# A recommendation tower: gathers released by step counts, 32x128 unit matmuls, and an opening whose ids are spread by matmuls

## What is computed

```python
e = jnp.stack([tbl_0[ids[:, 0]], ..., tbl_39[ids[:, 39]]], axis=1)
xi = inputs[:, iidx, :]
xj = inputs[:, jidx, :]
out = jnp.einsum('bpd,pde,bpe->bp', xi, bilinear_matrices, xj)
...
h = jnp.concatenate([z, dense_ctx], axis=1)
h = jnp.maximum(h @ W_top1 + b_top1, 0.0)
h = jnp.maximum(h @ W_top2 + b_top2, 0.0)
y = h @ W_top3
```

## Time and profile before

| | us |
|---|---|
| median of 3 runs | 1214.42 |
| span of the profiled execution | 1229.4 |
| PE busy | 958.3 (78%) |
| DVE busy | 556.3 (45%) |
| POOL busy | 470.2 (38%) |
| ACT busy | 175.3 (14%) |
| chain that ended last: PE | 73% |
| the same: "issue" | 16% |
| the same: another core or an unknown queue | 7% |

### The profile page before, as it was taken

The page is one execution under the profiler, slowest core; times in us unless marked ns, Lnnn a source line. Parts: engine busy times, 40 slices in busy tenths (PEclk is TensorE's granted clock), DMA queues, the critical chain, the costliest instruction groups (busy, mean ns, idle before and its releaser), DMA issues.

```text
span 1229.4 us, 30049 instructions
## 1 busy us (share of the span) xinstructions
PE 958.3 (78%) x13844; PEld 463.2 (38%) x13844; DVE 556.3 (45%) x652; ACT 175.3 (14%) x432; POOL 470.2 (38%) x502
## 2 busy tenths in 40 slices
PE   5136768878968778777788877888788877887998
PEld 4012334423435334433244323443234422344556
DVE  5013336524736445543255433553345623445782
ACT  3100001111102111211001110012101121012211
POOL 7745342453142442335422454226532265222000
PEclk9556687888878899889787887888888888888999
DMA  5006000010000100001000100001000000000000
GB/s 132 14 18 214 8 10 6 8 37 8 5 9 6 36 10 6 8 12 33 9 7 6 36 10 10 6 7 37 10 9 6 6 13 10 8 6 6 3 3 1
DMA packets 28094, 24.32 MB, mean 20 GB/s; under 512 B 11525, under 2 KB 25793, under 8 KB 27841
## 3 DMA queue, kind: packets, MB, share of 16 engines
q0 software_dynamic: 15616, 8.03, 4.3%
q1 hardware_dynamic: 11738, 13.87, 3.5%
q10 hardware_dynamic: 616, 0.51, 0.1%
HBM read 22.31 MB, written 0.06 MB: 18 GB/s over the span
## 4 chain that ended last, share of the span: by engine, by line
PE 73%; issue 16%; another core or an unknown queue 7%; ACT 2%; DVE 1%; SPq 1%; ACTq 0%; DMA 0%
PE Y L634 25%; PE ZL L654 23%; PE ZL L680 14%; PE H L610 8%; PE H L589 2%; ACT xcols L763 1%; PE Y L689 1%; DVE one L863 0%; PE Y L698 0%; PE H L593 0%; SPq L489 0%; ACTq L472 0%; PE H L689 0%; DMA tab<-tbl 0%
## 5 line engine op out<-in xcount | busy, mean ns | idle before, releaser
L560 POOL DMA_INDIRECT rows<-tbl,idx x488 | 468.7, 961 | 645.9 <-PE H L589 447.3
L894 DVE TENSOR_TENSOR prod<-Y,xcols 128x1024 f32<-128x1024 f32 x336 | 400.2, 1221 | 518.6 <-remote 399.4
L634 PE MATMUL Y<-xcols,mats 32*64 32x256 f32 x6400 | 334.6, 429 | 72.3 <-issue 40.8
L654 PE MATMUL ZL<-prod,sel 128*32 128x256 f32 x3200 | 316.3, 421 | 65.3 <-issue 59.5
L634 PEld LDWEIGHTS Y<-xcols,mats 32*64 32x64 f32 x6400 | 171.2, 146 | 233.6 <-issue 204.5
L680 PE MATMUL ZL<-z,w_sb 128*32 128x256 f32 x1568 | 169.6, 421 | 33.8 <-issue 29.8
L654 PEld LDWEIGHTS ZL<-prod,sel 128*32 128x32 f32 x3200 | 114.6, 117 | 213.4 <-issue 175.0
L763 ACT ACTIVATE xcols<-H 32x256 f32<-32x256 f32 (+3 forms) x219 | 82.5, 377 | 523.9 <-PE H L589 264.5
L610 PE MATMUL H<-one,parts 125*32 125x256 bf16 x1668 | 99.4, 317 | 70.3 <-issue 69.1
L680 PEld LDWEIGHTS ZL<-z,w_sb 128*32 128x32 f32 x1568 | 63.1, 116 | 114.2 <-issue 89.2
L610 PEld LDWEIGHTS H<-one,parts 125*32 125x32 bf16 x1668 | 54.8, 105 | 116.6 <-issue 112.6
(11 more groups left out here) (48 smaller groups left out, 152.4 us busy)
## 6 DMA issues: line engine op xcount, KB each, us to landing
rows<-tbl,idx POOLq DMA_INDIRECT x488
idb<-ids_turned SPq DMA_DIRECT2D x7, 768.0 KB
w_sb<-w SPq DMA_DIRECT2D x1, 1792.0 KB
mats<-m_wide SPq DMA_DIRECT2D x22, 64.0 KB
mats<-m_wide SPq DMA_DIRECT2D x1, 1152.0 KB
mats<-m_wide SPq DMA_DIRECT2D x1, 960.0 KB
idb<-ids_turned SPq DMA_DIRECT2D x12, 64.0 KB
tab<-tbl SPq DMA_DIRECT2D x6, 112.0 KB
```

The lines of the kernel that those rows point to most:

```text
L560: pool.indirect_dma_start(out=rows[:, slot, t, D * q:D * (q + 1)], out_offset=None, in_=tables[f], in_offset=bass.IndirectOffsetOnAxis(ap= ...
L634: last = pe.matmul(Y[2 * D * c:2 * D * (c + 1), bank, cols], mats[D * r:D * (r + 1), u * P + 2 * D * c:u * P + 2 * D * (c + 1)], xcols[D * ...
L654: last = pe.matmul(Z[D * q:D * (q + 1), :], sel[:, GF * (SPAN - 1 - o):GF * (SPAN - 1 - o) + 32], prod[:, (2 * s + bank_of(k, q) // 2) % P ...
L894: dve.tensor_tensor(prod[:, half, :, :].rearrange("p b (u c) -> p b u c", c=BLK), Y[:, pair:pair + 2, :].rearrange("p b (u c) -> p b u c", ...
```

## The change

- **Gathers.** A table `gather_steps` gives each gather a step, and POOL waits for `s_y` to reach it before that one gather. From block 1 on the steps are 0.43 apart and not earlier than half a step after the slot's last turn. In block 0 the first 12 gathers are free, the next 6 wait for the first hot look-ups, and the others are spread between earlier turns. POOL still issues in the order of blocks and waves.
- **Unit matmuls.** In the 21 steps of a block that hold no diagonal slot, `multiply` uses 8 matmuls of 32 rows and 128 columns in place of 16 of 64. The 4 others stay as they were. Operands and results are the same.
- **The opening.** Block 0's ids are spread by matmuls: a column of ids, repeated 128 times, times an identity matrix in fp16 (`widen`), copied by ACT to `idb` (`spread`). DVE's order is new: first 10 one-hot slots, then table parts between the others. PE's first hot look-ups go part by part, and the other blocks' ids are turned in steps 1 and 2 as fills, copied by ACT and loaded behind step 3.
- **Loads.** `mats` comes in pieces of three units about five steps ahead, `w1` tile by tile in steps 10 to 22, `w2` and the rest in step 23, each behind a wait of SP for `s_y`; later blocks' ids come in three loads in place of one.

The core of the diff:

```diff
-LOADS = [(0, 3), (3, 5), (5, 10), (10, 16), (16, 22), (22, 40), (40, NU)]
-
-BY_UNIT = 5
+LOADS = [(0, 3), (3, 5)] + [(u, min(u + 3, NU)) for u in range(5, NU, 3)]
+
+BY_UNIT = 2
+
+AHEAD = 5
+SPREAD_AT = 3
+SPREAD_BY = SPREAD_AT + 3
+DENSE_AT, W1_AT, W2_AT = 8, range(10, 24, 2), 23
+W_DMAS = ZT + 4
+
+
+def load_step(k):
+
+    return max(min(SLOT_OF[u] for u in range(*LOADS[k])) // PAIR - AHEAD, 0)
...
+GATHER_EVERY, LANDS_IN = 0.43, 3.0
+FREE_WAVES = 3
+
+IDS_AT = [1, 1, 2, 2]
...
-FIRST_SLOTS = 23
+FIRST_SLOTS = HOT_RING
...
+def gather_steps():
+
+    waves = [(n, j) for n in range(NB) for j in range(len(cold(n)))]
+    turned = {("turn", n, j): 0.0 for n, j in waves}
+    turned.update({what: float(s) for s, step in enumerate(ITEMS) for what in step if what[0] == "turn"})
+    at, t = [], 0.0
+    for k, (n, j) in enumerate(waves):
+        if (n, j) == (1, 0):
+            t = 0.0
+        count = BT * len(cold(n)[j])
+        for i in range(count):
+            if n == 0 and j < FREE_WAVES:
+                t = -2.0
+            elif n == 0:
+                a, b = [turned["turn", 0, j - d] if j - d >= FREE_WAVES - 1 else -1.0 for d in (2, 1)]
+                t = a + (b - a) * i / count if a >= 0 else -1.0
+            else:
+                free = turned[("turn", *waves[k - RING])]
+                t = max(t + GATHER_EVERY, free + 0.5)
+            at.append(t)
+        assert n == 0 and at[-1] < turned["turn", n, j] or at[-1] + LANDS_IN <= turned["turn", n, j], (n, j, at[-1], turned["turn", n, j])
+    return at
...
-            def spread_first(i):
-                for j in range(GF * i, GF * (i + 1)):
-                    sp.dma_start(idb[:, 0, j, :], ids_turned[0, j, :].partition_broadcast(P)).then_inc(s_first[i], DMA)
-
-            def spread_ids(n):
+            def spread_ids(n, i):
                 if n > 1:
                     sp.wait_ge(s_hot, hot_count(n - 1))
-                sp.dma_start(idb[:, n % 2, :, :], ids_turned[n].partition_broadcast(P)).then_inc(s_idb[n % 2], DMA)
-
-            sp.dma_start(idx[:, :, :], ids.rearrange("(p m) f -> p m f", p=P)).then_inc(s_idx, DMA)
+                sp.dma_start(idb[:, n % 2, GF * i:GF * (i + 1), :],
+                             ids_turned[n, GF * i:GF * (i + 1)].partition_broadcast(P)).then_inc(s_idb[n % 2], DMA)
...
+            by_sample = ids.rearrange("(p m) f -> p m f", p=P)
+            sp.dma_start(idx[:, 0:BT, :], by_sample[:, 0:BT, :]).then_inc(s_idx, DMA)
             load_tables(sp, 0)
-            sp.wait_ge(s_ids, 1)
-            sp.dma_start(ids_turned[0], idt[:, 0:BLK]).then_inc(s_idd, DMA)
-            sp.wait_ge(s_idd, DMA)
-            spread_first(0)
-            spread_first(1)
-            load_mats(0)
-            load_mats(1)
-            load_tables(sp, 2)
-            spread_first(2)
-            load_mats(2)
-            load_mats(3)
-            sp.wait_ge(s_rest_ids, 1)
-            load_mats(4)
-            sp.dma_start(ids_turned[1:NB].rearrange("n j c -> j n c"),
-                         idt[:, BLK:BATCH].rearrange("j (n c) -> j n c", c=BLK)).then_inc(s_idd, DMA)
-            sp.wait_ge(s_idd, 2 * DMA)
-            spread_ids(1)
-            sp.wait_ge(s_y, 1)
-            for k in range(5, len(LOADS)):
+            sp.dma_start(idx[:, BT:MT, :], by_sample[:, BT:MT, :]).then_inc(s_rest_idx, DMA)
+            for k in range(BY_UNIT):
                 load_mats(k)
+                if k == 1:
+                    load_tables(sp, 2)
             sp.wait_ge(s_const, 1)
-            load_dense(0)
-            sp.dma_start(w1_sb[:, :, :], w1.rearrange("(t p) n -> p t n", p=P)).then_inc(s_w, DMA)
-            sp.dma_start(w2_sb[:, :, :], w2.rearrange("(t p) n -> p t n", p=P)).then_inc(s_w, DMA)
-            sp.dma_start(w3_sb[:, :], w3).then_inc(s_w, DMA)
-            sp.dma_start(b1_sb[:, :], b1).then_inc(s_w, DMA)
-            sp.dma_start(b2_sb[:, :], b2).then_inc(s_w, DMA)
+            w1_tiles = w1.rearrange("(t p) n -> p t n", p=P)
+            for w in range(NS):
+                sp.wait_ge(s_y, 2 * w + 1)
+                for k in range(BY_UNIT, len(LOADS)):
+                    if load_step(k) == w:
+                        load_mats(k)
+                if w == SPREAD_AT:
+                    sp.wait_ge(s_free, PASS["ids", 0, len(IDS_AT) - 1] + 1)
+                    sp.dma_start(ids_turned[1:NB].rearrange("n j c -> j n c"),
+                                 idt[:, :].rearrange("j (n c) -> j n c", c=BLK)).then_inc(s_idd, DMA)
+                    sp.wait_ge(s_idd, DMA)
+                    for i in range(len(HOT)):
+                        spread_ids(1, i)
+                if w == DENSE_AT:
...
+                if w in W1_AT:
+                    t = W1_AT.index(w)
+                    sp.dma_start(w1_sb[:, t, :], w1_tiles[:, t, :]).then_inc(s_w, DMA)
+                if w == W2_AT:
...
+                first = sum(BT * len(cold(a)[b]) for a, b in waves[:k])
+                for i, f in enumerate(cold(n)[j]):
                     q = f % GF
                     for t in range(BT):
                         m = n * BT + t
+                        start = starts[first + BT * i + t]
+                        if start >= 0:
+                            pool.wait_ge(s_y, int(2 * start) + 1)
+                        elif start == -1.0:
+                            pool.wait_ge(s_used, sum(PLACES[h[2]] for h in HEAD if h[0] == "hot"))
                         pool.indirect_dma_start(
...
+            def widen(i):
+                if i == 2:
+                    pe.wait_ge(s_spread, 1)
+                flat = wide_ids(i).rearrange("p b c -> p (b c)")
+                for q in range(GF):
+                    for m in range(BT):
+                        c = (q * BT + m) * P
+                        last = pe.matmul(flat[:, c:c + P], idh[:, m, GF * i + q:GF * i + q + 1].to_broadcast([P, P]), eye[:, :],
+                                         start=True, stop=True, skip_group_check=True)
+                last.then_inc(s_wide, 1)
...
+            def look_up_first(i):
+                at = PASS["hot", 0, i]
+                for part in range(3):
+                    pe.wait_ge(s_cast, casts.index((i, part)) + 1)
+                    for t in range(PLACES[i]):
+                        v = hot_slot(0, i, t)
+                        if part == 0:
+                            pe.wait_ge(s_hot, v + 1)
+                        for q, f in enumerate(HOT[i]):
+                            c = TAB_AT[f] + t * D
+                            last = pe.matmul(stage(at)[D * q:D * (q + 1), :], parts[:, part, c:c + D], one[:, v, q, :],
+                                             start=t == 0 and part == 0, stop=t == PLACES[i] - 1 and part == 2,
+                                             skip_group_check=True)
+                        if part == 2:
+                            last.then_inc(s_used, 1)
...
                         cols = slice(half * BLK, (half + 1) * BLK)
-                        for c in range(2):
+                        wide = not any(on_diagonal(j) for j in slots(w))
+                        for c in range(1 if wide else 2):
+                            p0, p1 = (0, P) if wide else (2 * D * c, 2 * D * (c + 1))
                             for r in [r for r in range(GF) if bank_of(k, r) // 2 == pair]:
                                 u = SLOTS[k][1 if on_diagonal(k) and r > 2 * c else 0]
                                 bank = 2 * ((2 * s + pair) % 3) + bank_of(k, r) % 2
-                                last = pe.matmul(Y[2 * D * c:2 * D * (c + 1), bank, cols],
-                                                 mats[D * r:D * (r + 1), u * P + 2 * D * c:u * P + 2 * D * (c + 1)],
+                                last = pe.matmul(Y[p0:p1, bank, cols], mats[D * r:D * (r + 1), u * P + p0:u * P + p1],
                                                  xcols[D * r:D * (r + 1), n % 2, UNITS[u][1], :], start=True, stop=True,
...
+            pe.wait_ge(s_eye, 1)
+            pe.wait_ge(s_idh, 1)
+            for i in range(len(HOT)):
+                widen(i)
             pe.wait_ge(s_const, 1)
-            pe.wait_ge(s_idf, 1)
-            turn_ids(0, BT)
+            keep_clock()
             for what in HEAD:
-                if what == HEAD[1]:
-                    keep_clock()
-                if what[0] == "hot":
-                    pe.wait_ge(s_cast, casts.index((what[2], 2)) + 1)
                 fill(*what)
-                if what == ("hot", 0, 1):
-                    pe.wait_ge(s_ids, 1)
-                    pe.wait_ge(s_free, 2)
-                    turn_ids(BT, MT)
+            pe.wait_ge(s_spread, len(HOT))
             for n in range(NB):
                 for w in range(NS):
                     multiply(n, w)
-                    if (n, w) == (0, 0):
-                        pe.wait_ge(s_rest_ids, 1)
...
+            def spread(i):
+                act.wait_ge(s_wide, i + 1)
```

(28 more changed lines are left out.)

103 lines of the change are left out of this document (64 added, 39 removed).

## The result

On the chip of this result the changed kernel takes 926.99 us (median of 4 runs, 922.78 to 936.9) against 1215.83 us before (4 runs, 1207.89 to 1218.06): ratio 0.763, 95% interval 0.758 to 0.768 (the 936.9, a run in the slower of the two states in which these programs run, is left out of the ratio). The forecast was 1050, range 920 to 1200. The profiled execution took 922.78 us for a span of 921.0.

What follows compares the result with a forecast made beforehand. The prediction took PE, slowed by gathers at 1.19 us each (429 us for 360), to bound the kernel. Opening 33, block 0 180, blocks 1 to 6 738, block 7 97 and tail 17 gave 1065, less 15: 1050 us, range 920 to 1200.

Steps and rivals of the forecast that it cites:

- the forecast's own case: Whole kernel: a gather costs 0.45 to 0.95 us, total 945 to 1155 us; chance 0.58.
- rival A: Gathers among steps are nearly hidden, at 0.35 us each; total 875 us, chance 0.12.
- Opening: Time up to step 0's first product: from 88.9 us to 33, between 25 and 50, a change of -56.
- Block 0: First block: from 162.9 us to 180, +17, with 50 gathers in an unpaused run at 1.25 us each and 45 at 0.7.
- A single gather among steps: Paced gathers, 2.33 to a step: 0.7 us each in place of 1.19; blocks 1 to 6 at 123 us each, -147 in all.
- nearest row: Second window of a wave of gathers: 18 of 57 PE records, 1.7 us lost, 0.86 us per gather.
- The factor 0.81 for the wide matmuls: Price of a paced gather: wide unit matmuls take away 2688 of 13844 records, 19%, so 0.86 x 0.81 = 0.70 us.
- Wide matmuls at full pace: Unit matmuls over 168 steps: 0 us taken, bounds -13 and +39, since weight loads overlap.
- Waits of POOL and SP: Added waits on gathers and loads: cost nothing as long as a step lasts over 1 us.
- Rival B: Every gather costs 1.19 us, however placed; total 1194 us, chance 0.17.
- C: Rival: evenly spaced gathers keep PE's clock down, blocks at 162 us; total 1371 us, slower, chance 0.10.
- B': Rival: gathers are not the cause, blocks keep 147.4 us and only the opening gains; total 1158 us, chance 0.03.

Runs made afterwards that it cites:

- burst: The changed kernel without step gates on the gathers of blocks 1 to 7, which come in waves of 8 again; 1208.93 us, ratio to before 0.994.

## Why the prediction was right, and where it was off

The forecast's mechanism came true on the chip it was made for: faster, by gathers that cost less when they stand in twos and threes. Its size did not. The kernel gained 289 us where 164 were forecast, and 927 lies below the 945 to 1155 given for the forecast's own case, between it and rival A's 875. It was the wide range, down to 920, that held the result, and by 7 us only: there luck had a part. The sum was 144 us too high (1065 against a span of 921.0), and the experiments say where.

- *Opening, 33 forecast, 29.5 measured.* Right in size. But the working had it as a gain of its own (-56), and it is not: burst has it too, and gains 7.5 us in all. The old opening was long because of the 47 gathers in it; where nothing is slowed by gathers it takes 30.1 us. Moved away, they slowed block 0 instead, which the step on block 0 did charge.
- *Block 0, 180 forecast, 169.7 measured.* The run of overdue gathers came, 38 of them and not 50, and its price was near: 45 us for that step against 3.3 without gathers (the same step in later blocks), 1.10 each (1.25 forecast). Step 1's wait behind a second long run was not foreseen.
- *A single gather among steps, 0.70 forecast, 0.46 measured.* This is the mis-sized term. A block was to lose 41 us to 58 gathers and 6 to the clock, 123 in all, and takes 103.3: 6 x 19.7 = 118 of the 144 us. Block 7 and the end took 102.1 where 114 were forecast, 12 more. (The 0.46 has the clock in it; with its 6 us the forecast was 0.80 a gather.) The 0.86 of the "nearest row" was the second window of a wave, which already held a third gather, as the forecast's last sentence feared. By the step table a pair costs 0.34 each, a third and a fourth 1.1 to 1.2. The truth lies between that term and rival A's 0.35, nearer to A.
- *The factor 0.81 for the wide matmuls* held: 0.46 / 0.54 = 0.84, near the 19% fewer records. The width is worth 31.6 us where gathers are paced. In bursts it is worth next to nothing (146.4 us a block against 147.4), and where nothing slows PE, nothing.
- *Wide matmuls at full pace, 0 forecast:* blocks of 76.7 us wide and 76.6 narrow where gathers slow nothing. Right.
- *Waits of POOL and SP at nothing:* nothing in the runs speaks against it. Where steps are fast, the gates alone cost the kernel before 4 us (684.4 against 680.4).
- *The signs.* As forecast: the first product at 29.5 us, a clock of 0.97 to 1.00 in blocks 1 to 6, a full step of `multiply` in 1.16 us, DVE's unnamed waits at 2.2 us. Missed: blocks 1 to 6 at 101.1 to 106.1 us (110 to 135 forecast), the long run with 38 gathers (40 to 55), and its one wait of 35.8 us.
- *A reading.* The prediction has the clock of blocks 1 to 6 at 0.85 to 0.91; three of them stand at 0.84. The sum does not hang on it.
- *Rival B* (price by the gather, however placed) fell by the changed kernel against burst; *C* by the clock of 0.97 to 1.00. *B'* fell by the kernel without gathers, on that chip. On four other chips gathers slow PE nowhere, but there B' has nothing to save either: the kernel before takes 681 us, not 1158. What the Trainium skill says (SBUF — State Buffer, Who interferes with whom), that a DMA does not contend with a compute engine, agrees with the traces of those four (76.7 us a block with 62 gathers on the fifth) and disagrees with those of the first (103.3 with 58, 76.7 with none). No run shows in what the two would meet.

So the prediction read the profile rightly, and what the profile showed does not hold everywhere: where gathers slow TensorE the change is worth 24%, on the fifth chip nothing (1.000, 0.999 to 1.001).

**Open.** Why the first chip does this and four others do not. That it is the chip is itself not shown: no chip was measured twice, and all runs at 1216 us were made before all runs at 681, so a passing state of the machine would look the same. In the traces the gathers' issue time is the same. PE's records and the arrival of its results differ, and one thing more: each gather raises its semaphore by 16 in single increments, 7808 in all, and the trace of the fifth chip holds 7739 of them, that of the result 3285, that of the kernel before 2122. Increments that are missing there may be one reason for the unnamed waits. They also leave a rival standing that no run tests: every execution of the experiments has a span and a granted clock, so it was recorded as it was timed, and the recording itself may have a part in the slowing. Nor is it known which part of a gather does it (rows, indices or the instruction), whether the length of a run or the number in a step sets the price, or what single gathers 1.7 us apart would cost: the runs made for these questions fell on chips without the effect.

## What to carry to other kernels

Where one engine's pace falls with another's transfers and no wait names them, take those transfers out of a few blocks: that gives their full price in one run. Where transfers that follow each other without a pause cost more apiece than a pair alone, hold them apart by the program's steps, and count what a shorter opening only pushes on. Before tuning against a slowing that has no visible releaser, run the kernel before on a second chip, and on the first one once more later.
